# Every fourth key-value product on GpSimd, carried to PSUM by ScalarE

## What is computed

```python
x = x + layernorm(attn(layernorm(x)))
x = x + layernorm(ffn(x_after_attn := layernorm(x)))

# attn: 16 heads of 16 features; k is normalised inside each head
def step(F, q_t, k_t, v_t):                 # scan over the 512 tokens
    hebbian = einsum('bhd,bhe->bhde', v_t, k_t)
    F = retention * F + coef * hebbian      # retention, coef: [head, d, e]
    y_t = einsum('bhde,bhe->bhd', W_LTM + F, q_t)
# then y @ W_o.T

# ffn: h = relu(x @ W_fc.T)**2 ; y = h @ W_proj.T
# five steps of a spiking neuron driven by y; output = spikes / 5
```

## Time and profile before

| | us |
|---|---|
| median of 3 runs | 641.24 (640.99 to 642.02) |
| the profiled execution | 641.24 |
| its span in the trace | 639.4 |
| DVE busy | 547.7 (86%) |
| PE busy | 496.6 (78%) |
| POOL busy | 383.8 (60%) |
| ACT busy | 335.8 (53%) |

### The profile page before, as it was taken

The page is one execution under the profiler, slowest core; times in us unless marked ns, Lnnn a source line. Parts: engine busy times, 40 slices in busy tenths (PEclk is TensorE's granted clock), DMA queues, the critical chain, the costliest instruction groups (busy, mean ns, idle before and its releaser), DMA issues.

```text
span 639.4 us, 7834 instructions
## 1 busy us (share of the span) xinstructions
PE 496.6 (78%) x2248; PEld 325.9 (51%) x2256; DVE 547.7 (86%) x1024; ACT 335.8 (53%) x637; POOL 383.8 (60%) x181
## 2 busy tenths in 40 slices
PE   1674664479896999699969996999889987795891
PEld 0451333146663667266636573557556653383670
DVE  6899999998999999999999999999999999721001
ACT  4632113444556754775467547563665456546634
POOL 0347755885568757776687757775787577711101
PEclk9756589579997989799989999898979997987796
DMA  7555656364734764376446644555347644200000
GB/s 236 175 143 142 195 142 191 99 194 119 213 101 123 223 181 129 103 201 194 132 133 165 213 130 142 141 180 165 103 113 200 196 102 129 67 1 0 33 1 33
DMA packets 54730, 87.64 MB, mean 137 GB/s; under 512 B 5408, under 2 KB 19360, under 8 KB 54688
## 3 DMA queue, kind: packets, MB, share of 16 engines
q1 hardware_dynamic: 54112, 87.12, 47.3%
q10 hardware_dynamic: 576, 0.03, 0.1%
HBM read 78.74 MB, written 8.39 MB: 136 GB/s over the span
## 4 chain that ended last, share of the span: by engine, by line
PE 46%; issue 18%; DVE 15%; ACT 11%; POOL 9%; DMA 1%; POOLq 0%; ACTq 0%; DVEq 0%
PE p_c L344 13%; DVE state L689 9%; PE p_c L369 9%; PE p_a L279 5%; POOL prod L818 5%; PE p_y L322 5%; PE p_c L335 3%; DVE p_u L679 3%; ACT sign L522 3%; PE p_c L352 2%; PE p_a L299 2%; POOL x1t L834 2%; PE p_y L317 2%; ACT oo L449 2%; DVE stats L643 1%
## 5 line engine op out<-in xcount | busy, mean ns | idle before, releaser
L818 POOL TENSOR_TENSOR prod<-state,qf 128x1024 f32<-128x1024 f32 x128 | 302.7, 2369 | 148.4 <-DVE state L689 130.1
L689 DVE TENSOR_TENSOR_SCAN state<-ret,p_u 128x512 f32<-128x512 f32 x256 | 309.9, 1211 | 0.0
L679 DVE TENSOR_TENSOR p_u<-vrep,p_k 128x512 f32<-128x512 f32 x256 | 172.0, 678 | 0.5 <-ACT p_k L454 0.5
L344 PE MATMUL p_c<-wproj_sb,ht 128*128 128x256 f32 x512 | 116.3, 382 | 1.9 <-ACT ht L512 1.4
L344 PEld LDWEIGHTS p_c<-wproj_sb,ht 128*128 128x128 f32 x512 | 95.5, 190 | 25.6 <-issue 11.5
L369 PE MATMUL p_c<-x1t,wfc_s 128*128 128x512 f32 x384 | 98.3, 407 | 8.2 <-POOL x1t L834 7.1
L279 PE MATMUL p_a<-xt,wqkv_s 128*128 128x512 f32 x276 | 85.3, 449 | 11.9 <-POOL xt L834 4.2
L369 PEld LDWEIGHTS p_c<-x1t,wfc_s 128*128 128x128 f32 x384 | 72.9, 193 | 31.5 <-POOL x1t L834 12.1
L322 PE MATMUL p_y<-prod,summer 128*32 128x512 f32 x512 | 76.2, 670 | 9.2 <-POOL prod L818 9.2
L279 PEld LDWEIGHTS p_a<-xt,wqkv_s 128*128 128x128 f32 x276 | 55.1, 210 | 45.2 <-issue 15.2
L352 PE MATMUL p_c<-sign,ident_b 128*128 128x512 bf16 x72 | 25.6, 500 | 39.5 <-ACT sign L522 38.5
(11 more groups left out here) (95 smaller groups left out, 502.4 us busy)
## 6 DMA issues: line engine op xcount, KB each, us to landing
vrep<-v_rows SPq DMA_DIRECT2D x256, 256.0 KB, 3.5
xa<-in_x SPq DMA_DIRECT2D x8, 512.0 KB, 5.2
v_rows<-vf SPq DMA_DIRECT2D x16, 256.0 KB, 2.1
x<-in_x SPq DMA_DIRECT2D x8, 512.0 KB, 4.4
out<-x SPq DMA_DIRECT2D x8, 512.0 KB, 2.9
prod<-in_w_fc SPq DMA_DIRECT2D x1, 1024.0 KB, 7.2
wproj_sb<-in_w_proj SPq DMA_DIRECT2D x1, 1024.0 KB, 9.6
state<-in_w_qkv SPq DMA_DIRECT2D x1, 512.0 KB, 5.1
```

Source lines behind the costliest of these rows:

```text
L344: last = pe.matmul(p_c[(u + 1) % 2][:, 0:D], ht[:, f, tokens(u)], wproj_sb[:, f, :], start=(f == 0), stop=(f == FT - 1))
L679: v.tensor_tensor(p_u[n % NU][:, :], vrep[:, n % NV, :], p_k[:, :], ALU.mult).then_inc(S["hebb_done"], 1)
L689: v.tensor_tensor_scan(state[:, s % NS, i, :], ret[:, r:r + 1].broadcast_to([P, L]), p_u[n % NU][:, :], 0.0, ALU.mult, ALU.add).then_inc(S ...
L818: p.tensor_tensor(prod[:, s % NZ, :, :], state[:, s % NS, :, :], qf[:, s // HS, :].unsqueeze(1).broadcast_to([P, 2, L]), ALU.mult).then_in ...
```

## The change

Of every four products, the fourth (n % 4 == 3, that is the second product of each odd slot) is made by POOL: `pool_hebbian`, in the even slot before, after `read`, multiplies `vrep` by the key tile `kf` into an SBUF tile `us` (two buffers). ACT copies it to the bank `p_u` where the scan expects it (`move_u`, at the head of each odd slot). DVE leaves out these products and waits for `u_moved` before their scans. `kf` gets one tile per half, since POOL now reads it while the next one may be written. SP waits for POOL's count instead of DVE's where POOL was the last reader of the `vrep` buffer.

```diff
--- before.py
+++ after.py
@@ -66,6 +66,18 @@
     return s // HS, (first, first + 4)
 
 
+def on_pool(n):
+
+
+    return n % 4 == 3
+
+
+def before_on_vector(n):
+
+
+    return n - (n + 1) // 4
+
+
 def build(nc, x, w_qkv, w_o, w_fc, w_proj, w_ltm, head_params, shared_params, ident, head_mask, pick, out):
     ctx = ExitStack()
     with ctx:
@@ -118,7 +130,8 @@
         kdev = sb("kdev", [P, TILES * HH])
         krd = sb("krd", [P, TILES * HH])
         krx = sb("krx", [P, TILES, DK, HH])
-        kf = sb("kf", [P, L])
+        kf = sb("kf", [P, HALVES, L])
+        us = sb("us", [P, 2, L])
         qf = sb("qf", [P, HALVES, L])
         vf = sb("vf", [P, HALVES, L])
         vrep = sb("vrep", [P, NV, L])
@@ -155,7 +168,7 @@
             setup_ready setup_exp centred wv_high wv_low wk_high wk_low wq_high wq_low wide_high wide_low tables_done setup_step
             n1_stats n1_var n1_dev n1_step n1_done  xt_turned xt_done xt_high xt_low
             k_proj k_sq k_var k_dev k_rdev k_spread k_scale k_done k_bank  v_proj v_done  q_proj q_done
-            v_out hebb_done state_done prod_done sum_done y_done
+            v_out pool_hebb_done u_moved hebb_done state_done prod_done sum_done y_done
             o_proj o_done n2_stats n2_var n2_dev n2_step n2_done x1_done
             n3_stats n3_var n3_dev n3_step n3_done  x1_turned x1t_done x1t_high x1t_low
             up_done relu_done h_done down_done yf_done
@@ -230,7 +243,10 @@
                     sp.wait_ge(S["v_out"], 16 * (2 * b + half + 1))
                 for i, d in enumerate(features):
                     n = 2 * (SLOTS * b + s) + i
-                    sp.wait_ge(S["hebb_done"], at(n - NV + 1))
+                    if on_pool(n):
+                        sp.wait_ge(S["pool_hebb_done"], at(n // 4 - 1))
+                    else:
+                        sp.wait_ge(S["hebb_done"], at(before_on_vector(n - NV) + 1))
                     rows = v_rows[(2 * b + half) % 4, d * HH:(d + 1) * HH, :]
                     sp.dma_start(vrep[:, n % NV, :], rows.unsqueeze(0).broadcast_to([DK, HH, L])).then_inc(
                         v_in[n % NV], 16)
@@ -483,8 +499,13 @@
                 copy(p_a[:, :], vf[:, half, :], "v_proj", 2 * b + half + 1, "v_done")
 
             def copy_key(b, half):
-                act.wait_ge(S["hebb_done"], DK * (2 * b + half))
-                copy(kf[:, :], p_k[:, :], "k_done", 2 * b + half + 1, "k_bank")
+                act.wait_ge(S["hebb_done"], before_on_vector(DK * (2 * b + half)))
+                copy(kf[:, half, :], p_k[:, :], "k_done", 2 * b + half + 1, "k_bank")
+
+            def move_u(b, s):
+                n = 2 * (SLOTS * b + s) + 1
+                act.wait_ge(S["state_done"], at(n - NU + 1))
+                copy(us[:, n // 4 % 2, :], p_u[n % NU][:, :], "pool_hebb_done", n // 4 + 1, "u_moved")
 
             def copy_q(b, half):
                 act.wait_ge(S["prod_done"], at(SLOTS * (b - 1) + HS * (half + 1)))
@@ -556,6 +577,7 @@
             def iteration(g, now, before, two_before, after):
                 b, b1, b2 = g + 1, g - 1, g - 2
                 for s in range(SLOTS):
+                    if now and s % 2 == 1: move_u(g, s)
                     if s == 0:
                         if now and before: copy_key(g, 0)
                         if after: deviation(1, b)
@@ -667,8 +689,9 @@
 
             def norm_k(b, half):
                 dve.wait_ge(S["k_scale"], at(2 * b + half + 1))
-                dve.wait_ge(S["k_bank"], at(2 * b + half))
-                v.tensor_tensor(kf[:, :], p_a[:, :], kc[:, :], ALU.mult).then_inc(S["k_done"], 1)
+                dve.wait_ge(S["k_bank"], at(2 * (b - 1) + half + 1))
+                dve.wait_ge(S["pool_hebb_done"], at(HS // 2 * (2 * (b - 1) + half + 1)))
+                v.tensor_tensor(kf[:, half, :], p_a[:, :], kc[:, :], ALU.mult).then_inc(S["k_done"], 1)
 
             def hebbian(b, s, i):
                 n = 2 * (SLOTS * b + s) + i
@@ -683,7 +706,10 @@
                 half, features = step_features(s)
                 r = half * DK + features[i]
                 n = 2 * (SLOTS * b + s) + i
-                dve.wait_ge(S["hebb_done"], n + 1)
+                if on_pool(n):
+                    dve.wait_ge(S["u_moved"], n // 4 + 1)
+                else:
+                    dve.wait_ge(S["hebb_done"], before_on_vector(n) + 1)
                 if i == 0:
                     dve.wait_ge(S["prod_done"], at(SLOTS * b + s + 1 - NS))
                 v.tensor_tensor_scan(state[:, s % NS, i, :], ret[:, r:r + 1].broadcast_to([P, L]),
@@ -790,7 +816,7 @@
                     if before and s == 8: scales(3, b1)
                     if now:
                         if first: hebbian(g, s, 0)
-                        hebbian(g, s, 1)
+                        if s % 2 == 0: hebbian(g, s, 1)
                         scan(g, s, 0)
                     if after and s == 2: scales(1, b)
                     if now and s == 4: key_reciprocal(g, 1)
@@ -819,6 +845,15 @@
                                 qf[:, s // HS, :].unsqueeze(1).broadcast_to([P, 2, L]), ALU.mult).then_inc(
                     S["prod_done"], 1)
 
+            def pool_hebbian(b, s):
+                half = s // HS
+                n = 2 * (SLOTS * b + s) + 1
+                pool.wait_ge(v_in[n % NV], 16 * (n // NV + 1))
+                pool.wait_ge(S["k_done"], at(2 * b + half + 1))
+                pool.wait_ge(S["u_moved"], at(n // 4 - 1))
+                p.tensor_tensor(us[:, n // 4 % 2, :], vrep[:, n % NV, :], kf[:, half, :], ALU.mult).then_inc(
+                    S["pool_hebb_done"], 1)
+
             def add_attention(b):
                 pool.wait_ge(S["n2_done"], at(TILES * (b + 1)))
                 pool.wait_ge(S["again_in"], at(16 * (b + 1)))
@@ -849,6 +884,7 @@
                 for s in range(SLOTS):
                     if s > 0 and now: read(g, s - 1)
                     if s == 0 and before: read(b1, SLOTS - 1)
+                    if now and s % 2 == 0: pool_hebbian(g, s + 1)
                     if before and s == 6: add_attention(b1)
                     if after and s in (7, 9): low_x(b, (s - 7) // 2)
                     if before and s == 10:
```

## The result

The changed kernel takes 658.12 us (656.5 to 658.98), the kernel before 641.37 in the same comparison: ratio 1.025, 95% interval 1.0224 to 1.0276. It is slower by 16.8 us; the forecast was 652, in the range 636 to 662. The profiled execution has a span of 657.0 us against 639.4.

What follows compares the result with a forecast made beforehand. PE and ScalarE, with a GpSimd stop, were taken to bound batches 2 to 6, VectorE's loop nearly as long. From 641.2 us, +14 in the middle and -3.5 in the other batches gave 652, range 636 to 662.

Steps and rivals of the forecast that it cites:

- (a): Middle batches: `move_u(1)` on ScalarE between `hidden(7)` and `kc` delays `ksq`, for which PE waits: +0.5 us a batch.
- (b): Middle batches: `move_u(7)` on ScalarE between `copy_yf(2)` and `dev` 3 delays the signs, for which PE waits: +0.5 us a batch.
- Term (c): Middle batches: late scans and product(11) on GpSimd before `low_x1` delay it and PE: +1.15 us, between +0.45 and +2.4.
- E + 15.6: Forecast end of `low_x1`, 15.6 us after E, the end of `move_u(7)`; the loop took 14.4 us from `dev`.
- Term (d): Middle batches: scan (13,1) behind `norm` 4, then product(15) and its move, delay `hidden(5)`, whose relu frees `up(7)`'s bank: +0.5 us.
- The sum of the middle: Batches 2 to 6: four terms, +2.65 us a batch on a loop of 67.5, about +14 us with the batches' two lengths.
- Batches 0 and 1: Outer batches where VectorE's saving counts: -2.7 us in batch 0, -0.8 in batch 1; together with batch 7, -3.5.
- Rival 1: The queues take the new work in their gaps, (c) and (d) are nothing: faster, 632 us; chance 0.17.
- rival 2: The ceiling, VectorE's loop rules everywhere: 604 us; chance 0.04 together with the rest.
- rival 3: Nothing much changes: (c) only 0.45 us, (d) gone, 634 to 645 us; chance 0.17.
- Rival 4: Slower still: with each move PE's low clock comes oftener or lasts longer, +8 us, 660; chance 0.12.
- 684: Time in us by the skill's engine rule alone: 641 plus 80 of GpSimd work less 37 of VectorE work.

Runs made afterwards that it cites:

- without slots 11 and 15: Changed kernel with the products of slots 11 and 15 back on VectorE, 48 of 64 left on GpSimd: 646.8 us, ratio 1.007 to the kernel before.
- the two runs with loads alone: Kernel before plus extra ScalarE copies in odd slots, 649.98 us; kernel before plus extra GpSimd products in even slots, 649.41 us; nothing taken from VectorE.

## Why the prediction was right, and where it was off

**The bound** (PE and ScalarE set the pace in five batches, VectorE is only level with them): right, shown by the run without the 64 products, whose period does not move in the mean and by 0.55 us in two of the batches. It is also where the shares of the earlier trace rows mislead most: 86% busy, and 35 us less work is worth 10.

**Terms (a) and (b)**: right. PE's wait for `ksq` went from 1.43 to 1.94 to 1.96 us, that for the signs from 5.24 to 5.74.

**Term (c)**: right in mechanism and nearly in size. E + 15.6 was forecast; it is 15.7 from the end of `move_u(7)` at 328.8 to 344.47. The term is 1.3 for 1.15, and moving product (11) behind `low_x1` removes it.

**Term (d)**: right in mechanism, forecast at half its size. Scan (11,1) waits 3.45 us behind `hidden(0)`, (13,1) 1.50 behind `norm` 4, and `up(7)` waits for the relu of `hidden(5)`. The timeline after:

```profile
361.84 1.29 POOL L854 TENSOR_TENSOR us<-vrep,kf 128x512 f32<-128x512 f32 x1
...
363.22 0.59 ACT L470 COPY p_u<-us 128x512 f32<-128x512 f32 x1 [2.32 <-POOL us L854]
363.75 0.59 ACT L531 ACTIVATE hr<-p_c 128x512 f32<-128x512 f32 x1
...
364.48 1.64 PE L385 MATMUL p_c<-x1t,wfc_s 128*128 128x512 f32 x6 [0.51 <-ACT hr L531]
```

PE idles 0.51 us where 0.5 was forecast, but this is the batch that the low clock had already made late. In the other four PE idles for 0.70 to 0.73 us there, and the stretch from `low_x1` to `project_out` is 0.95 longer for it: 28.3 us, and 27.4 without slots 11 and 15.

**The sum of the middle**: forecast +14 for five batches, measured +17.1. The four terms measure 0.5, 0.5, 1.3 and 0.95, 3.25 us a batch for the 2.65 of the forecast. That is 3.0 of the 3.1 missing, and most of it is (d). Beyond the terms the forecast had added 0.9 for batches of two lengths, with a 337 that its own figures don't give (3 x 67.5 + 2 x 66.2 = 334.9); with them it would have been 650, a little further off. Measured, 0.9 stands there all the same, from other things: 2.1 us more in the one batch with `project_k` at the low clock, about 1 less between `project_out` and `dev`, where the times of `project_out` differ and VectorE's work comes earlier. The move of slot 3 costs nothing here: in the changed kernel `down(0)` waits for `copy_o` in no middle batch.

**Batches 0 and 1**: forecast -3.5, measured -1.9, of which -1.8 in batch 0 (forecast -2.7). What batch 0 lacks is open. In batch 1 I applied `add_attention` and `low_x1`, but not what I had found for the middle, that scan (11,1) stands behind `hidden(0)`. There it is worst of all, 6.5 us (waits of VectorE in batch 1):

```profile
DVE state L715 <- ACT p_u L470: 6.5, 1, 6.5
DVE stats L665 <- POOL x L860: 0.9, 1, 0.9
```

The second line is the 0.9 us for `add_attention` that was forecast.

**Behind the middle**: forecast 0, measured +2.3. It is term (d) again, in batch 7. From one `project_out` to the next the changed kernel takes 63.7 us there and the kernel before 59.7. ScalarE waits for product(15), `hidden(5)` stands behind its move, and PE waits for the relu before `up(7)`, which it did not do before (timeline after):

```profile
572.84 2.90 PE L385 MATMUL p_c<-x1t,wfc_s 128*128 128x512 f32 x6 [4.41 <-ACT hr L531]
```

Without slots 11 and 15 this wait is gone and the same distance is 58.5 us. The prediction had this chain in batch 7 and gave it 1.5 us.

In all, 658 lies inside the stated 636 to 662 and one microsecond above the 647 to 657 that the forecast gave itself.

**The rivals**: none held as a whole. Rival 1 (gaps take the work) fails by the two runs with loads alone, +7.3 and +6.6; rival 2 by the run without the products; rival 3 by (c) and (d), which are 1.3 and 0.95. Rival 4, the low clock, fails too: `project_out` takes no longer in the mean than before (4.56 us for 4.71), and the loss is the same with PE's waits filled. What the prediction set down for this rival, that of the batches 4 and 5 only one is followed by a slow `project_out`, was misread: both are (5.39 and 5.38 us), and the one behind batch 3, with the same 5.24 us of idle time, is not. Taking engine time for time, the prediction's other sum, 684 was to be expected; GpSimd's and ScalarE's extra time is 110 us, and 17 appeared.

## What to carry to other kernels

Before moving work off the busiest engine, leave it out altogether and look at the period: here the run without the 64 products would have said that no place for them could gain more than 10 us. When work goes into an in-order queue, its price is set by the instruction behind it and not by the engine's share: one product put two instructions later gave back half of the loss. And before a difference of periods is explained, count how often the clock was low in either: here that alone moved a period by 0.6 us. Last, a copy that hands a result from one engine to another couples three queues at once; it belongs where the instruction ahead of it in its queue does not itself wait.

## What the runs showed of the hardware that I had not expected

- Ten matmuls of no use in a 5.2 us wait of PE made the kernel 0.9% faster. The five behind them took 2.31 us in every middle batch before, at a granted clock of 0.52, and 1.25 to 2.32 us after, 1.25 at 1.00. Behind one and the same 2.7 us of idle time that were left over, one kernel had both.
- PE kept the high clock behind 1.5 to 2.0 us of idle time in four batches of the changed kernel and had the low one 1.5 us after an idle time of 2.1 in the fifth.
- A GpSimd product of 128x512 from SBUF takes 1277 ns with two different inputs and 1042 ns with one tile as both.
- A ScalarE copy of 128x512 from SBUF takes 584 ns into PSUM and 609 ns into SBUF.
